# Order of the transposes in the middle stage of a two-expert-layer transformer block: zn behind the sums over queries, hn beside kv, x2 beside the sums

## Reference, cut to what matters

```
x = q_x                                    # 8 x 512 x 256, 4096 tokens of 256
x = x + 0.5 * experts(layernorm(x))        # switch layer, 8 experts, capacity 256 tokens each
x = x + attention_block(layernorm(x))      # the middle
x = x + 0.5 * experts(layernorm(x))

attention_block(y):
    xn = ln(y, ln1);  q, k, v = xn @ wq + bq, xn @ wk + bk, xn @ wv + bv
    fq, fk = elu(q) + 1, elu(k) + 1        # 16 heads of 16; sums over the heads of ONE token
    kv = einsum('bhnd,bhne->bnde', fk, v);  k_sum = fk.sum(heads)
    attn = einsum('bhnd,bnde->bhne', fq, kv) / (fq . k_sum + 1e-6)
    x1 = y + attn @ wo + bo
    h = gelu(ln(x1, ln2) @ fc_w + fc_b)    # 256 -> 1024
    return x1 + h @ proj_w + proj_b

experts(y): logits = y @ w_switch + b; the best expert of each token; a token's place is the count of
    earlier tokens with the same expert; kept if place < 256; kept tokens go through their expert,
    the others pass; times pmax / stop_gradient(pmax)
```

## Time and profile before

| what | value |
|---|---|
| median of 3 runs | 734.08 us (733.74 to 734.09) |
| the profiled execution | 733.78 us, with a span of 732.0 us from first to last instruction |
| busy share of the span | PE 92%, PE weight load 78%, DVE 65%, ACT 57%, POOL 45% |
| mean granted TensorE clock | 0.97 of full |
| the chain that ended last, by engine | PE 74%, DVE 7%, issue 6%, POOL 3%, ACT 3%, DMA 3% |

### The profile page before, as it was taken

How to read it: one execution, slowest core, us unless ns; L and a number is a source line. 1 busy time by engine, 2 the same in 40 slices (tenths; PEclk the granted TensorE clock), 3 DMA queues, 4 the chain that set the end, 5 groups by cost and what they waited for, 6 DMA issues and landing times.

```text
span 732.0 us, 17446 instructions
## 1 busy us (share of the span) xinstructions
PE 673.8 (92%) x6214; PEld 569.1 (78%) x6214; DVE 478.5 (65%) x1332; ACT 419.6 (57%) x841; POOL 326.8 (45%) x493
## 2 busy tenths in 40 slices
PE   7689999998777999999999999999999886999994
PEld 5449999975555788888888888888888662999994
DVE  7856657425577676767777868677676565776751
ACT  5755555503233767676767667666754642767660
POOL 5252564122133453545564664745547564253412
PEclk9879999999999999999999999999999996999998
DMA  8479687414666454534554555454443344466730
GB/s 266 149 251 311 222 283 259 136 39 99 102 101 102 74 87 74 110 66 82 100 90 82 115 85 130 66 110 87 87 73 98 112 134 116 139 220 220 222 94 29
DMA packets 287103, 95.56 MB, mean 131 GB/s; under 512 B 213988, under 2 KB 284736, under 8 KB 287018
## 3 DMA queue, kind: packets, MB, share of 16 engines
q1 hardware_dynamic: 270666, 85.38, 47.5%
q0 software_dynamic: 3840, 8.32, 3.6%
q10 hardware_dynamic: 12512, 0.76, 1.1%
HBM read 65.09 MB, written 29.40 MB: 129 GB/s over the span
## 4 chain that ended last, share of the span: by engine, by line
PE 74%; DVE 7%; issue 6%; POOL 3%; ACT 3%; DMA 3%; ACTq 2%; SPq 1%; POOLq 0%; DVEq 0%
PE bank L1711 67%; PE bank L1720 7%; ACTq L373 2%; POOL hids L782 1%; SPq L367 1%; DMA qkv_rows<-feats 1%; POOL xb_rows L677 1%; DMA xb_rows<-late_rows,xb_token 1%; ACT hids L1016 1%; DMA x_all<-in_L_attn_q_x_dram 1%; ACT feats L986 1%; POOL table L665 1%; DMA keys<-qkv_rows 0%; ACT ots L1039 0%; DVE att_ L1552 0%
## 5 line engine op out<-in xcount | busy, mean ns | idle before, releaser
L1711 PE MATMUL bank<-down_w,hids 128*128 128x256 f32 x768 | 105.8, 286 | 1.9 <-POOL hids L782 1.6
L1711 PE MATMUL bank<-hnts,up_w 128*128 128x512 f32 x384 | 104.5, 407 | 0.0
L782 POOL TENSOR_TENSOR hids<-hid,hids 128x512 fp32r<-128x512 f32 x64 | 83.1, 1299 | 41.8 <-ACT hids L1016 41.6
L1711 PEld LDWEIGHTS bank<-down_w,hids 128*128 128x128 f32 x768 | 95.7, 188 | 6.1 <-POOL hids L782 3.3
L1711 PE MATMUL bank<-qkv_w,xnts 128*128 128x256 f32 (+1 forms) x384 | 76.8, 348 | 5.0 <-DVE xnts L1565 4.0
L1711 PEld LDWEIGHTS bank<-hnts,up_w 128*128 128x128 f32 x384 | 67.5, 189 | 11.5
L1711 PEld LDWEIGHTS bank<-qkv_w,xnts 128*128 128x128 f32 x384 | 61.1, 191 | 17.3 <-DVE xnts L1565 6.6
L1013 ACT ACTIVATE hid<-bank,cols 128x512 f32<-128x512 f32 x64 | 44.0, 687 | 45.9 <-PE bank L1711 45.6
L773 POOL TENSOR_SCALAR sth<-sth 128x1 f32<-128x1 f32 x32 | 7.2, 224 | 129.1 <-DVE sth L1577 129.0
L1711 PE MATMUL bank<-a_w,xa_h 128*128 128x256 f32 x256 | 60.1, 379 | 0.0
L1711 PE MATMUL bank<-xa_xt,a_w 128*128 128x256 f32 x384 | 55.1, 294 | 1.4 <-DVE xa_xt L1303 1.4
(11 more groups left out here) (272 smaller groups left out, 1536.2 us busy)
## 6 DMA issues: line engine op xcount, KB each, us to landing
qkv_rows<-feats SPq DMA_DIRECT2D x32, 384.0 KB, 3.1
a_raw<-in_L_ffn_w_dram SPq DMA_DIRECT2D x32, 256.0 KB
a_w<-in_L_ffn_w_dram SPq DMA_DIRECT2D x32, 256.0 KB
b_raw<-in_L_ffn_w_dram SPq DMA_DIRECT2D x32, 256.0 KB
b_w<-in_L_ffn_w_dram SPq DMA_DIRECT2D x32, 256.0 KB
mid_rows<-x_all SPq DMA_DIRECT2D x8, 512.0 KB
x<-mid_rows SPq DMA_DIRECT2D x32, 128.0 KB, 2.5
values<-qkv_rows SPq DMA_DIRECT2D x32, 128.0 KB
```

What stands on the lines that cost most here:

```text
L782: pool.tensor_tensor(hids[1][u % 3][:], hid[u % 2][:], f32(hids[0][u % 3][:]), ALU.subtract).then_inc(s_hidl, 1)
L1711: return pe.matmul(dst, left, right, start=start, stop=stop, skip_group_check=True)
```

## The change

On the PE, zn's turn goes from the top of a step to the end of the step before (`at(s, 2)` at the top becomes `at(s, 1)` behind `sum_att`, the x2 turns and the statements for half 1), so only `count` and `down_mid` of its step come after it. hn's turn goes ahead of `project`, right behind `turn_kv`. The x2 turns of half 0 go from ahead of `project` to right behind `sum_att`, next to those of half 1, and from bank B_TURN to bank B_V. On ACT the copy of half 0's x2 tiles follows, behind the second pair of gelus. Nothing is added or removed; tiles, banks' number and DMAs are as before. The order on DVE, POOL and SP is not touched.

```diff
 # ACT
                     help_queries(s - 3)
-                for n in turned_at(s, 0):
-                    features(n, bank[B_TURN])
                 if at(s, 6) is not None:
                     turn_h(s - 6)
                 if 0 <= g_up < NG:
                     gelus(g_up, 2 * j_up + 1)
+                for n in turned_at(s, 0):
+                    features(n, bank[B_V])
                 for n in turned_at(s, 1):
                     features(n, bank[B_KV])
 # PE
             for s in range(MID_STEPS):
-                n = at(s, 2)
-                if n is not None:
-                    dst = bank[B_TURN]
-                    pe.wait_ge(s_zn, n + 2)
-                    if turn_free:
-                        pe.wait_ge(*turn_free)
-                    for k in range(KD):
-                        last = turn(dst[:, k * P:(k + 1) * P], zn[:, k * P:(k + 1) * P])
-                    last.then_inc(s_znt, 1)
-                    turn_free = (s_xnl, n + 1)
                 if 0 <= g_up < NG:
                     up_mid(g_up, 2 * j_up)
...
                     turn_kv(s - 4)
                     kv_free = (s_kv, s - 3)
-                for n in turned_at(s, 0):
-                    pe.wait_ge(*turn_free)
-                    turned(n, bank[B_TURN])
-                    turn_free = (s_bfeat, n + 1)
-                if at(s, 5) is not None:
-                    pe.wait_ge(*v_free)
-                    project(s - 5)
-                    v_free = (s_xo, s - 4)
                 n = at(s, 6)
                 if n is not None:
...
                     last.then_inc(s_hnt, 1)
                     turn_free = (s_hnl, n + 1)
+                if at(s, 5) is not None:
+                    pe.wait_ge(*v_free)
+                    project(s - 5)
+                    v_free = (s_xo, s - 4)
                 if 0 <= g_up < NG:
                     up_mid(g_up, 2 * j_up + 1)
...
                 if at(s, 4) is not None:
                     sum_att(s - 4)
+                for n in turned_at(s, 0):
+                    pe.wait_ge(*v_free)
+                    turned(n, bank[B_V])
+                    v_free = (s_bfeat, n + 1)
                 for n in turned_at(s, 1):
                     pe.wait_ge(*kv_free)
                     turned(n, bank[B_KV])
                     kv_free = (s_bfeat, n + 1)
+                n = at(s, 1)
+                if n is not None:
+                    dst = bank[B_TURN]
+                    pe.wait_ge(s_zn, n + 2)
+                    if turn_free:
+                        pe.wait_ge(*turn_free)
+                    for k in range(KD):
+                        last = turn(dst[:, k * P:(k + 1) * P], zn[:, k * P:(k + 1) * P])
+                    last.then_inc(s_znt, 1)
+                    turn_free = (s_xnl, n + 1)
                 g = routed(s, 1)
```

## The result

The changed kernel takes 735.89 us (median of 9 runs, 734.64 to 737.1), beside 733.95 us for the kernel before (9 runs). The ratio is 1.0026, with a 95% interval of 1.0013 to 1.0038: slower by 1.9 us, half a microsecond above the forecast of 735.4 us. It is also above the 735.55 us where the prediction drew the line to slower, a case that it had given 0.35 against 0.50 for no change.

What follows compares the result with a forecast made beforehand. PE's work and few waits were taken to bound steps 10 to 33. Waits +3.4, their steps -0.4, plain -0.4, x2 -0.3, ACT's copies -0.8, step 10 -0.2: +1.3 on 734.08, so 735.4 us; range 732.3 to 736.9 us.

Steps and rivals of the forecast that it cites:

- What bounds the middle: Steps 10 to 33: PE's own work and few waits set the time, at full clock; plain step 11.95 us.
- zn's turn waits in five steps: Steps 14, 18, 22, 26, 30: zn's turn waits for low_h behind add_rest, +3.4 us; their savings -0.4 us.
- The shift of 0.22 us: hn's turn ahead of the projection delays xo and low_h, making each of five waits 0.22 us longer.
- One sign: Expected in the profile after: xo 0.99 us behind the projection and 1.2 us behind kv's turn.
- The free restart: Rival, chance 0.05: the waiting turn's weight load runs ahead, each of five waits 0.16 us shorter; 734.6 us.
- The small gains: Cheaper places for turns on PE win 0.03 to 0.09 us a step: add_rest -0.4, plain -0.4, x2 steps -0.3.
- The x2 steps: Ten steps with x2 turns, 15, 16, 19, 20, up to 32: some 0.03 us won each, 0.3 us in all.
- Step 10: hn's turn fits into the projection's 1.38 us wait for the copy of v: 0.23 us won.
- The rival without these gains: Turns cost the same at new neighbours as at old, so 0.4 + 0.4 + 0.3 us aren't won: 736.5 us, chance 0.22.
- ACT's copies: Steps 20, 24, 28, 32: hn's turn no longer waits for ACT's copy of the x2 tile, -0.8 us.
- What the split of x2's turns wins: Moving x2's turns to B_V removes a 0.20 us wait in steps 20, 24, 28, 32: 0.8 us won.
- Steps up to 9, and step 39: Both put at 0; bounds: up to 1.5 us won in steps 6 to 9, 0.37 us lost in step 39.

Runs made afterwards that it cites:

- the kernel with low_h first: The changed kernel with DVE making low_h ahead of add_rest; 734.38 us, ratio 1.0002 to the kernel before.
- zn alone: The kernel before with only zn's turn moved behind the sums over queries, hn's and x2's turns as before; 735.85 us, ratio 1.0031.
- all but step 39: The changed kernel with step 39's first two x2 tiles turned at their old place, in B_TURN; 735.73 us, ratio 1.0031.
- the kernel with hn and x2 alone: The kernel before with hn's turn and the x2 turns of groups 0 to 5 moved, zn's turn and step 39 as before; 733.83 us, ratio 0.9995.

## Why the prediction was right, and where its sum was off

**What bounds the middle.** Right. PE's busy time and its idle time account for the whole difference, and the granted clock stayed at 1.00 there in all profiles.

**zn's turn waits in five steps.** Right in mechanism, place and number. 0.60 and 0.73 us of lost time were forecast, 3.4 in all less 0.4; the steps grew by 0.51, 0.61, 0.73, 0.72 and 0.72 us, 3.3 us net against 3.0. zn's turn alone makes most of the loss, and the kernel with low_h first, which has the changed order without the wait, isn't told from the kernel before.

**The shift of 0.22 us.** Right, and shown: 0.20 to 0.22 us a step between zn alone and all but step 39. One sign was misadded: xo was to come 1.2 us behind kv's turn, but 0.35 + 0.22 + 0.99 make 1.56, and step 14 has 1.57 (290.86 to 292.43 us). What I didn't see is that the same shift delays add_rest for the down_mid, by 0.05 to 0.18 us a step in the kernel with hn and x2 alone. It costs the changed kernel nothing, since its turn waits longer, but it is the next wait when zn's is removed. The free restart didn't come: the turn starts 0.15 us behind low_h, as the earlier trace rows had it. The rule of the Trainium skill that weight loads may be pulled ahead ("TensorE: Matmul & The Clock Gate", "Step-by-step: what each phase is for") doesn't show in this wait, where the turn's load began at 295.29 us, 0.12 us behind low_h's end.

**The small gains.** Right. Plain steps became 0.05 to 0.08 us shorter each where I had 0.05. The x2 steps gave 0.3 as forecast, but not through zn's turn: with zn alone they are as long as before (12.37 and 12.82 us). Step 10 gave 0.29 us where I had 0.23 and its plain 0.05. The rival without these gains forecast 736.5 us, which lies inside the interval of the measured time (734.9 to 736.7 us); the lengths of the steps rule it out, not the median.

**ACT's copies.** The step of the sum that failed. "What the split of x2's turns wins" put 0.8 us on the extra 0.20 us in steps 20, 24, 28 and 32. Those steps have it in the first profile of the kernel before alone; all later ones with this order have step 20 at 12.81 to 12.83 us. There ACT's copy is done in time and hn's turn comes 0.80 us behind the projection, as in step 12. The x2 turns moved alone left the middle at 295.89 us, 0.2 below the kernel before. Without this term the sum is +2.1 us and the forecast 736.2 us; the measured ratio means +1.9 (1.0 to 2.8). So the term didn't help: the forecast held because 0.8 us is small beside its range. The next user of B_V behind an x2 step is the second switch's logits, at the top of the step, and not the v products as the prediction has it; it shows no wait for ACT either.

**Steps up to 9, and step 39.** Steps 4 to 9 together took 55.2 to 56.3 us in the five profiles of the two kernels, too uneven for an effect of up to 1.5 us. Step 9 by itself speaks for nothing gained: ACT's copy of hn comes 2.11 us behind ACT's last work in the changed kernel and 2.14 in the kernel before, low_h waits 0.34 us for it where it waited 0.37, and zn's turn stands 3.03 us behind the projection where it stood 3.07. Step 39 without a fall of the clock is even (19.14 against 19.13 us), as worked out.

## What to carry to other kernels

A product that stands between two others may be the cover of the second one's wait: before moving it, follow what the next instruction asks for, in every kind of step, the periodic extra work above all. Here seventeen steps won 0.02 to 0.08 us each and step 10 0.3, and five lost 0.5 to 0.7. A term of 0.2 us read from one profile should be looked for in a second profile of the same kernel before it is multiplied. And a row of turns that hand a bank back and forth pays for each copy between them: more banks won more here than any order of the turns.

## What the runs showed of the hardware that was not expected

- Idle gaps of 1.40 and 0.52 us between step 39's transposes were followed by 3.4 us at the 1.2 GHz level in two profiles and by none in four others with the same gaps: the same instruction stream can meet either clock.
- The copies that wait for PE's transposes, ACT's of an x2 tile and DVE's of kv, began late together four times in one execution, at the same place of steps 20, 24, 28 and 32, and each of these steps was 0.20 us longer; no other profile has it. A repeated delay is no proof that it belongs to the kernel.
- The granted clock also falls to 0.50 somewhere between 190 and 230 us, ahead of step 10, in every profile, but not at the same place: in the three of the changed kernel at 193, 217 and 200 us, for 3.4 us each. Their spans, 735.3, 732.4 and 733.1 us, vary by more than the change costs; 1.6 us of that is the fall in step 39, and the rest wasn't traced.
